# A grouped convolution taken two groups at a time, with its matmuls in turn into two PSUM banks

## What is computed

```python
def conv(x, c, weight, c_weight, bias):          # layers 0 and 3: 4 groups, 9 taps, padding 4
    out = lax.conv_general_dilated(x, weight, window_strides=(1,), padding=[(4, 4)],
                                   dimension_numbers=('NCH', 'OIH', 'NCH'), feature_group_count=4)
    return out + jnp.einsum('nd,od->no', c, c_weight)[:, :, None] + bias[None, :, None]

def mixed(x, embedding, W0, b0, W1, b1, W2, b2, weight, bias_k):     # layers 1 and 2: 8 experts
    h = jax.nn.gelu(embedding @ W0 + b0, approximate=False)
    h = jax.nn.gelu(h @ W1 + b1, approximate=False)
    att = jax.nn.softmax(h @ W2 + b2, axis=-1)
    agg_w = jnp.einsum('bk,koi->boi', att, weight[..., 0])
    return jnp.einsum('boi,bih->boh', agg_w, x) + (att @ bias_k)[:, :, None]

x = x + conv(x, cond, L0...);  x = x + mixed(x, cond, L1...)
x = x + mixed(x, cond, L2...); x = x + conv(x, cond, L3...)
```

## Time and profile before

| | us |
|---|---|
| median of 3 runs | 2578.09 |
| lowest and highest | 2578.03, 2578.33 |
| the profiled execution, its own time | 2577.78 |
| its span in the profile | 2575.7 |
| TensorE busy | 2550.1 (99%) |
| weight loads on TensorE, beside the matmuls | 2069.8 (80%) |
| ScalarE busy | 2100.5 (82%) |
| VectorE busy | 1955.4 (76%) |

### The profile page before, as it was taken

How to read it: one execution, slowest core, us unless ns; L and a number is a source line. 1 busy time by engine, 2 the same in 40 slices (tenths; PEclk the granted TensorE clock), 3 DMA queues, 4 the chain that set the end, 5 groups by cost and what they waited for, 6 DMA issues and landing times.

```text
span 2575.7 us, 42996 instructions
## 1 busy us (share of the span) xinstructions
PE 2550.1 (99%) x11068; PEld 2069.8 (80%) x11068; DVE 1955.4 (76%) x5032; ACT 2100.5 (82%) x1937; POOL 16.1 (1%) x29
## 2 busy tenths in 40 slices
PE   8999999999999999999999999999999999999998
PEld 6888888888888888888888888888888888888886
DVE  8777777777777777777777777777777777777774
ACT  6888888888888888888888888888888888888885
POOL 2000000000000000000000000000000000000000
PEclk9999999999999999999999999999999999999999
DMA  7888888888888888888888888888888888888876
GB/s 254 316 320 317 318 319 319 315 318 323 318 312 321 323 318 313 320 324 316 315 320 323 315 317 319 322 317 316 320 320 317 317 319 319 316 318 322 317 297 237
DMA packets 334986, 809.31 MB, mean 314 GB/s; under 512 B 37370, under 2 KB 39426, under 8 KB 302210
## 3 DMA queue, kind: packets, MB, share of 16 engines
q1 hardware_dynamic: 332736, 807.69, 84.3%
q10 hardware_dynamic: 2242, 1.53, 0.2%
HBM read 137.97 MB, written 134.23 MB: 106 GB/s over the span
## 4 chain that ended last, share of the span: by engine, by line
PE 98%; DMA 1%; DVE 1%; ACT 0%; SPq 0%; issue 0%; DVEq 0%; ACTq 0%
PE pair L877 82%; PE quad L927 14%; PE pair L917 1%; DMA x_ch<-x_ph 0%; DVE partial L701 0%; DMA mix<-att_saved 0%; DMA x_ph<-in_small 0%; SPq L269 0%; SPq L321 0%; SPq L294 0%; DMA att_saved<-att 0%; ACT x_out L569 0%; ACT x_ch L422 0%; DVE x_hi L734 0%; ACT x_ph L575 0%
## 5 line engine op out<-in xcount | busy, mean ns | idle before, releaser
L877 PE MATMUL pair<-x_hi,w_hi 128*128 128x512 f32 x3072 | 1227.7, 400 | 2.9 <-DVE x_lo L752 1.2
L877 PE MATMUL pair<-x_hi,w_lo 128*128 128x512 f32 x3072 | 1213.5, 395 | 0.0
L877 PE MATMUL pair<-x_lo,w_hi 128*128 128x512 f32 x3072 | 1209.2, 394 | 0.0
L877 PEld LDWEIGHTS pair<-x_hi,w_lo 128*128 128x128 f32 x3072 | 579.7, 189 | 137.5
L877 PEld LDWEIGHTS pair<-x_lo,w_hi 128*128 128x128 f32 x3072 | 582.0, 189 | 131.7
L877 PEld LDWEIGHTS pair<-x_hi,w_hi 128*128 128x128 f32 x3072 | 579.0, 188 | 131.3 <-DVE x_lo L752 1.6
L484 ACT ACTIVATE x_ph<-pair,bias_now 128x512 f32<-128x512 f32 x512 | 351.2, 686 | 254.8 <-PE pair L877 254.7
L422 ACT COPY x_ch<-x_in 128x1024 f32<-128x1024 f32 x255 | 528.3, 2072 | 0.0
L475 ACT COPY x_out<-x_ch 128x1024 f32<-128x1024 f32 x252 | 517.3, 2053 | 0.0
L493 ACT ACTIVATE x_ph<-pair,bias_now 128x512 f32<-128x512 f32 x508 | 355.5, 700 | 191.3 <-PE pair L877 191.3
L734 DVE CAST x_hi<-x_ch 128x512 fp32r<-128x512 f32 x512 | 204.9, 421 | 325.9 <-DMA x_ch<-x_ph 325.9
(11 more groups left out here) (83 smaller groups left out, 772.9 us busy)
## 6 DMA issues: line engine op xcount, KB each, us to landing
x_ph<-x_ch SPq DMA_DIRECT2D x1024, 256.0 KB, 2.5
x_ch<-x_ph SPq DMA_DIRECT2D x1024, 256.0 KB, 2.6
x_in<-in_x SPq DMA_DIRECT2D x128, 1024.0 KB, 5.6
out<-x_out SPq DMA_DIRECT2D x128, 1024.0 KB, 4.3
x_out<-in_W SPq DMA_DIRECT2D x8, 144.0 KB, 3.9
expert<-in_e ACTq DMA_DIRECT2D x2, 512.0 KB, 8.1
mix<-att_saved SPq DMA_DIRECT2D x2, 512.0 KB, 6.3
x_ph<-in_small ACTq DMA_DIRECT2D x1, 458.5 KB, 3.4
```

The costliest lines, as they stand in the source:

```text
L877: mm = nc.tensor.matmul(conv_bank[g % 2], w[l][:, m, g, :], x[:, g, m:m + N], start=(m == 0 and x is hi and w is w_hi), stop=(m == BLK - 1 ...
```

## The change

Two groups of a conv are taken together: the matmuls of groups 0 and 1 alternate, each group in its own bank, and then those of groups 2 and 3. `conv_bank` gets four banks, 0, 1, 6 and 7, one for each group. Bank 6 is also the middle matrix's, so `middle_matrix` now waits until group 2 of the conv two places earlier has been evacuated, and the second pair of conv1 waits until VectorE has copied the middle matrix. A pair waits for both its groups (x3 split, banks evacuated) before its first matmul. Two small uses of PSUM at the start move to `quad`. ScalarE, VectorE and SyncE keep their order.

```diff
-        conv_bank = bank[0:2]
+        conv_bank = [bank[n] for n in (0, 1, 6, 7)]
...
-        vec_ps = pair[1][:, :, 0:K // 2 * B]
+        vec_ps = quad[:, PH // 2:, 0:K // 2 * B]
...
-                nc.scalar.activation(x4_ph[:, g, :], conv_bank[g % 2], ACT.Identity,
+                nc.scalar.activation(x4_ph[:, g, :], conv_bank[g], ACT.Identity,
...
-            def conv(l, g, hi, lo, done):
+            def conv_pair(l, first, hi, lo, done):
                 for m in range(BLK):
                     for w, x in ((w_hi, hi), (w_hi, lo), (w_lo, hi)):
-                        mm = nc.tensor.matmul(conv_bank[g % 2], w[l][:, m, g, :], x[:, g, m:m + N],
-                                              start=(m == 0 and x is hi and w is w_hi),
-                                              stop=(m == BLK - 1 and w is w_lo))
-                mm.then_inc(done, 1)
+                        for g in (first, first + 1):
+                            last = m == BLK - 1 and w is w_lo
+                            mm = nc.tensor.matmul(conv_bank[g], w[l][:, m, g, :], x[:, g, m:m + N],
+                                                  start=(m == 0 and x is hi and w is w_hi), stop=last)
+                            if last:
+                                mm.then_inc(done, 1)
...
+            def conv1(b, firsts=range(0, G, 2)):
                 if not isinstance(b, int) or b >= 2:
                     pe.wait_ge(x_lo_ready, b - 1)
+                for first in firsts:
 
                     if isinstance(b, int) and b == 0:
+                        pe.wait_ge(x_lo_first, first + 2)
                     elif isinstance(b, int) and b == 1:
+                        pe.wait_ge(x_lo_second, first + 2)
+                        pe.wait_ge(x1_ready, first + 2)
                     else:
+                        pe.wait_ge(x4_ready, G * (b - 2) + first + 2)
+                    if first == G // 2 and not (isinstance(b, int) and b <= 1):
+                        pe.wait_ge(m_ready, b + 1)
+                    elif first == G // 2 and b == 1:
+                        pe.wait_ge(m_ready, 1)
+                    conv_pair(0, first, x_hi, x_lo, conv1_done)
+
+            def conv4(b, firsts=range(0, G, 2), after_x4=False):
+                for first in firsts:
+                    pe.wait_ge(x3_split, G * b + first + 2)
+
+                    if after_x4:
+                        pe.wait_ge(x4_ready, G * (b - 1) + first + 2)
+                    else:
+                        pe.wait_ge(x1_ready, G * (b + 1) + first + 2)
+                    if not after_x4 and first == G // 2 and isinstance(b, int) and b == 0:
+                        pe.wait_ge(m_ready, 2)
+                    conv_pair(1, first, x3_hi, x3_lo, conv4_done)
...
             def middle_matrix(b):
...
                 wait(pe, m_ready, b)
+                if isinstance(b, int) and b <= 1:
+                    pe.wait_ge(x1_ready, G * b + G // 2 + 1)
+                else:
+                    pe.wait_ge(x4_ready, G * (b - 2) + G // 2 + 1)
```

More of the change, by code:

```diff
@@ L483, in evacuate_x1 @@
                 act.wait_ge(conv1_done, G * b + g + 1)
-                nc.scalar.activation(x1_ph[:, g, :], conv_bank[g % 2], ACT.Identity,
+                nc.scalar.activation(x1_ph[:, g, :], conv_bank[g], ACT.Identity,
                                      bias=bias1_now[:, g:g + 1]).then_inc(x1_ready, 1)
@@ L794, in _ @@
             dve.wait_ge(bias3_done, 1)
-            nc.vector.tensor_copy(bias3_ch[:, :], bank[7][:, 0:B]).then_inc(bias3_all, 1)
+            nc.vector.tensor_copy(bias3_ch[:, :], bank[5][:, 0:B]).then_inc(bias3_all, 1)
             set_bias3(0)
@@ L882, in conv1 @@
-            def conv1(b, groups=range(G)):
+                        for g in (first, first + 1):
[5 more added lines that the diff above has]
+            def conv1(b, firsts=range(0, G, 2)):
@@ L883, in conv1 @@
                 if not isinstance(b, int) or b >= 2:
                     pe.wait_ge(x_lo_ready, b - 1)
-                for g in groups:
+                for first in firsts:
                     if isinstance(b, int) and b == 0:
[L888 to L892, removed]
-                    elif isinstance(b, int) and b == 1:
[L894 to L907, removed]
-                    else:
-                        pe.wait_ge(x1_ready, G * (b + 1) + g + 3)
-                    conv(1, g, x3_hi, x3_lo, conv4_done)
+                        pe.wait_ge(x_lo_first, first + 2)
+                    elif isinstance(b, int) and b == 1:
+                        pe.wait_ge(x_lo_second, first + 2)
+                        pe.wait_ge(x1_ready, first + 2)
+                    else:
+                        pe.wait_ge(x4_ready, G * (b - 2) + first + 2)
@@ L938, in _ @@
             pe.wait_ge(w_lo_ready, PH)
-            conv1(0, range(G // 2))
+            conv1(0, [0])
             pe.wait_ge(bias1_all, 1)
@@ L945, in _ @@
             expert_vectors()
-            conv1(0, range(G // 2, G))
+            conv1(0, [G // 2])
             pe.wait_ge(vec_weighted, 2)
@@ L952, in _ @@
             pe.wait_ge(turn_ready, 1)
-            nc.tensor.matmul(bank[7][:, 0:B], turn[:, :], bias3[:, :], start=True,
+            nc.tensor.matmul(bank[5][:, 0:B], turn[:, :], bias3[:, :], start=True,
                              stop=True).then_inc(bias3_done, 1)
@@ L965, in _ @@
             conv1(B - 1)
-            conv4(B - 2, range(G // 2))
+            conv4(B - 2, [0])
             middle(B - 1)
-            conv4(B - 2, range(G // 2, G))
+            conv4(B - 2, [G // 2])
             conv4(B - 1, after_x4=True)
```

## The result

| | before | after |
|---|---|---|
| median, us | 2578.06 (2577.18 to 2578.33, 4 runs) | 2668.26 (2666.92 to 2670.35, 4 runs) |
| ratio to before | | 1.0352 (95%: 1.034 to 1.0365) |
| span of the profiled execution | 2575.7 | 2664.9 |

The changed kernel is 3.5% slower, 90 us. The profiled execution took 2666.92 us; its span is 89.2 longer than before.

A forecast was written before the change was run, and what follows sets the result against it. PE bounds the kernel at 19.76 us a step; the change closes a chain through ScalarE and VectorE of 12.61 + 0.20 + 5.00 + 2.29 + 0.10 = 20.20. 2577.78 + 54.6 + 2.0 gives 2634 us, range 2590 to 2675.

The forecast's parts named there:

- the sum with the high bounds: Whole turn with each term at its upper bound: a step of 20.44 us, so 2664 us.
- the ends: First and last batches: nothing at the first, later x3, evacuations and middle matrix at the last; together 2.0 us.
- the slack of 1.81: Kernel before: 1.81 us between the first group's x3 split being ready and the first conv4 matmul needing it.
- Evacuations: ScalarE's x4 evacuations: first conv4 group ends 8 matmuls later, +1.86 us, plus +0.10 for PE's slower restart.
- The gap at the jump: VectorE, bias copy to middle-matrix copy: gap shrinks from 0.89 to 0.20 us, bounds 0.07 and 0.34.
- The far end of 0.89: VectorE's gap between bias copy and middle-matrix copy stays 0.89 us: step 20.99, so 2732 us; chance 0.01.
- The second x3 group: First conv4 pair waits for both groups' x3 split on VectorE; the first is ready 0.93 us earlier.
- What else is new fits: Other new waits (second conv1 pair, product, x3 transfer, x1 evacuation) end before PE's turn; x3 transfer cover 0.5 us.
- Within 19.76: Rival: the loop closes within PE's step and only the ends are left, 2580 us; chance 0.11.
- Cheaper matmuls: Rival: turning between banks makes PE's matmuls cheaper, 2545 us at the 0.188 floor; chance 0.08, of it 0.05 faster.
- Dearer: Rival: turning between banks costs PE 0.007 us a matmul, 0.5 us a step, so 2647 us; chance 0.04.
- The clock falls: Rival: PE's idling drops the granted clock to 0.50 for 12 matmuls each step, +298, 2878 us; chance 0.01.

The follow-up runs named there:

- Four copies: Four unread 128x128 copies added on VectorE between splitting the middle matrix and the mixing: kernel before 2577.3 us, changed kernel 2739.59 us.
- a jump of 4.04 us: Kernel before with VectorE's loop over five batches for one jump instead of one: 2613.11 us (1.0139).
- three kernels with a step of 19.80: Changed kernel with VectorE's conv4 bias copy after the mixing, 2589.05 us; ScalarE's first half cut before the first x4 evacuation, 2586.86; with the two edits together, 2586.72.
- the loop of five: Changed kernel with VectorE's loop over five batches for one jump instead of one: 2757.19 us (1.0689).
- both moves: Changed kernel with VectorE's conv4 bias copy after the mixing and ScalarE's first half of the cut before the first x4 evacuation: 2586.72 us (1.0039).
- fifteen: Kernel before with fifteen unread 128x128 copies on VectorE between splitting the middle matrix and the mixing: 2645.57 us (1.0264).

## Why the prediction was right

The direction, the mechanism and the place were right, and 2668 is in the range of 2590 to 2675, near its upper end; of the 90 us I had forecast 56. That it is in the range is in part luck: the sum with the high bounds gave 2664, and no sum stood behind the last 11 us up to 2675. Term by term, from the turn shown above:

| term | predicted | measured |
|---|---|---|
| conv4 pair's start to the bias copy | 12.61 | 1013.45 to 1025.94: 12.49 |
| bias copy to the middle-matrix copy | 0.20 | 1025.94 to 1026.43: 0.49 |
| to the first cast of x3 | 5.00 | 1026.43 to 1031.43: 5.00 |
| to the end of the second low part | 2.29 | 1033.04 + 0.69 - 1031.43: 2.30 |
| to PE's start | 0.10 | 1033.73 to 1033.86: 0.13 |
| the turn | 20.20 | 20.41, every other one 20.49; mean 20.455 |
| PE's own step | 19.76 | 19.80 when nothing waits |
| the ends | 2.0 | 3.0 |

**What bounds it, and the slack of 1.81.** Right. Four copies fit into the slack without a trace, a jump of 4.04 us stood out by what the slack left of it.

**Evacuations.** Right: the first x4 evacuation starts 1017.69 - 1013.45 = 4.24 after the pair, where it was 2.38. These are two different kinds of turn, though; by the mean of 110 steps it is 4.28 against 2.35, 1.93 more: the 8 matmuls (1.86) and 0.07. The restart is in that: from 1013.45 to 1014.02 two matmuls take 0.57, not 0.47. The term came out 0.12 lower in this turn and 0.03 lower in the other, whose evacuation starts 0.08 later.

**The gap at the jump was the term mis-sized.** I took 0.20 and an upper bound of 0.34, from the entry of the loop. There the loop is only entered and nothing jumps back, so the row bounded another thing. The jump back costs 0.39 over the 0.10 without it. 124 x 0.29 = 36 us, which covers all of what was missing (34); the other terms together came out a little under what I took. The far end of 0.89, which I gave a chance of 0.01, was the bound from the rows that held.
The Trainium skill's 108 ns for a compare-and-branch (Advanced Engine Details and Errata, Control Flow Timing) is not what a waiting engine pays here: the measurement, 0.39 us, decides.

**The second x3 group, 0.93 of the turn.** The wait is there and its length right. No run takes it away alone.

**What else is new fits.** Right: PE has no wait at conv1, at the second conv4 pair or at the product in the steady state. All its 124 waits of this kind are for the low part of x3.

**The rivals.** *Within 19.76* fell: each term counted. *Cheaper matmuls* fell: alternating made them dearer by 0.6 ns, in three kernels with a step of 19.80. *Dearer* was right in sign, a twelfth of the size I gave it as a bound, and hidden in the changed kernel itself. *The clock falls* fell: it is granted in full in all slices, with PE idle for 0.4 us at a time. In other versions it did fall, after stops of 1.6 to 2.6 us (the loop of five, and the ends); in the changed kernel's steady state no stop is that long. The Trainium skill's rule on cycling through PSUM banks (TensorE: Matmul & The Clock Gate, A second HAM failure mode) does not show in the changed kernel, where the bank changes at every conv matmul.

## What to carry to other kernels

An engine that is 99% busy can still sit within 2 us of a closed chain through the others. Before delaying one of its results, such as by finishing two accumulations together, follow who waits for the result all the way round to that engine and compare the length of the turn with the step. Where the turn is too long, moving one waiting instruction that others queue behind (here a bias copy of 0.17 us) gives back nearly all. And a gap that a wait covers has no price in the trace; bound it by the wait's full length.

## What the runs showed of the hardware

- The jump at the end of VectorE's loop costs 0.39 us more than no jump where nothing hides it (0.49 against 0.10), with a body of one or two batches; with a body of five it costs 3.9 (4.04 against 0.11), and the instruction queue moves 127 packets instead of 5.
- The granted clock fell to 0.50 after PE had stood idle for 2.58 us, in 15 of 24 rounds of the loop of five, and matmuls of 128x512 were then 0.43 apart instead of 0.23; after an equal stop of 2.56 us in another round it stayed at 1.00. Such a fall cost about 1.5 us. After a stop of 1.7 us both were seen too: it fell with both moves (1.68) and stayed up in the changed kernel (1.67).
- Two banks in turn, matmul by matmul, cost TensorE 0.04 us in 72 conv matmuls of 128x512 (19.80 against 19.76 a step); they save nothing.
- Copies of 128x128 in fp32 without dependence start 0.135 us apart on VectorE (four in 0.54, fifteen in 2.03), though each lasts some 0.22 (0.63 for the four, less three distances).
